# Decoder cross-attention: score matmuls and output copies issued in another order

## What is computed

```python
def _L1_xattn_ref(query, key, value, mask, Wq, bq, Wk, bk, Wv, bv, Wo, bo):   # key = value = ctx_1024
    q = (query @ Wq + bq).reshape(b, -1, H, HD).transpose(0, 2, 1, 3)
    k = (key @ Wk + bk).reshape(b, -1, H, HD).transpose(0, 2, 1, 3)
    v = (value @ Wv + bv).reshape(b, -1, H, HD).transpose(0, 2, 1, 3)
    scores = jnp.einsum('bhsd,bhtd->bhst', q, k) / jnp.sqrt(jnp.asarray(HD, q.dtype))
    scores = jnp.where(keep[None, None], scores, neg)
    w = jax.nn.softmax(scores, axis=-1)
    out = jnp.einsum('bhst,bhtd->bhsd', w, v)
    return out.transpose(0, 2, 1, 3).reshape(b, -1, D) @ Wo + bo
x = x + _L1_xattn_ref(_layernorm(x, axis=-1), ctx_1024, ctx_1024, mask_SxS2_ik0, ...)
```

## Time and profile before

| | |
|---|---|
| median of 3 runs | 3188.79 us (3188.61 to 3189.98) |
| the profiled execution, its own time | 3191.41 us |
| span of its trace | 3189.6 us |
| instructions | 37762 |
| PE busy | 2897.8 us (91% of the span) |
| DVE busy | 1304.7 us (41%) |
| ACT busy | 981.8 us (31%) |
| POOL busy | 247.2 us (8%) |

### The profile page before, as it was taken

The page is one execution under the profiler, slowest core; times in us unless marked ns, Lnnn a source line. Parts: engine busy times, 40 slices in busy tenths (PEclk is TensorE's granted clock), DMA queues, the critical chain, the costliest instruction groups (busy, mean ns, idle before and its releaser), DMA issues.

```text
span 3189.6 us, 37762 instructions
## 1 busy us (share of the span) xinstructions
PE 2897.8 (91%) x15710; PEld 2000.6 (63%) x15710; DVE 1304.7 (41%) x1979; ACT 981.8 (31%) x1469; POOL 247.2 (8%) x250
## 2 busy tenths in 40 slices
PE   7868899896998879999999979999999999987787
PEld 3336446354574458888888848778877877844422
DVE  3445363555741433333333342443344244246201
ACT  3233223123440234333443322332342243232100
POOL 1100110220000000000000011011101101000000
PEclk9989999997999979999999979999999999988899
DMA  9763794851021022222322210100100100021197
GB/s 385 289 274 109 306 378 188 357 225 40 14 76 47 24 80 94 104 92 94 104 92 93 104 69 21 44 23 21 44 24 21 44 24 21 24 113 40 57 422 298
DMA packets 62273, 388.87 MB, mean 122 GB/s; under 512 B 5696, under 2 KB 12096, under 8 KB 32704
## 3 DMA queue, kind: packets, MB, share of 16 engines
q1 hardware_dynamic: 26640, 190.57, 16.2%
q0 software_dynamic: 29024, 192.23, 15.3%
q10 hardware_dynamic: 6480, 4.20, 0.4%
HBM read 381.72 MB, written 5.24 MB: 121 GB/s over the span
## 4 chain that ended last, share of the span: by engine, by line
PE 68%; issue 10%; DMA 8%; DVE 8%; ACT 4%; POOL 2%; SPq 0%; DVEq 0%; ACTq 0%; POOLq 0%
PE PS L410 9%; PE PS L412 9%; PE PS L411 9%; PE PS L589 4%; PE PS L1644 4%; DMA PR<-in_ctxN 4%; PE PS L1625 3%; PE PS L1608 3%; PE PS L1626 3%; PE PS L1627 3%; PE PS L1610 3%; PE PS L1609 3%; PE PS L297 2%; DMA ring<-in_experts 2%; PE PS L564 2%
## 5 line engine op out<-in xcount | busy, mean ns | idle before, releaser
L410 PE MATMUL PS<-X_high,W_high 128*128 128x512 f32 x576 | 226.3, 393 | 14.5 <-DVE X_low L1124 7.3
L411 PE MATMUL PS<-X_low,W_high 128*128 128x512 f32 x576 | 225.8, 392 | 0.0
L412 PE MATMUL PS<-X_high,W_part 128*128 128x512 f32 x576 | 225.7, 392 | 0.0
L1106 DVE TENSOR_TENSOR W_part<-ring,W_high 128x2048 fp32r<-128x2048 f32 x63 | 147.0, 2334 | 188.6 <-ACT W_high L1072 188.6
L410 PE MATMUL PS<-H_high,W_high 128*128 128x512 f32 x576 | 224.1, 389 | 0.0
L411 PE MATMUL PS<-H_low,W_high 128*128 128x512 f32 x576 | 224.1, 389 | 0.0
L412 PE MATMUL PS<-H_high,W_part 128*128 128x512 f32 x576 | 224.1, 389 | 0.0
L1072 ACT ACTIVATE W_high<-ring 128x2048 fp32r<-128x2048 f32 x71 | 135.1, 1915 | 255.0 <-PE PS L412 255.0
L1808 DVE TENSOR_TENSOR RB<-PS,rows 128x512 f32<-128x512 f32 x104 | 71.9, 691 | 307.3 <-PE PS L1627 307.3
L1112 DVE TENSOR_TENSOR H_low<-T,H_high 128x512 fp32r<-128x512 f32 x144 | 99.7, 692 | 213.5 <-ACT H_high L1093 213.5
L1608 PE MATMUL PS<-C_high,W_part 128*128 128x384 f32 (+2 forms) x512 | 177.5, 347 | 4.9 <-DVE W_part L1780 4.9
(11 more groups left out here) (312 smaller groups left out, 5615.7 us busy)
## 6 DMA issues: line engine op xcount, KB each, us to landing
ring<-in_experts SPq DMA_DIRECT2D x96, 1024.0 KB, 4.9
ring<-in_tiles SPq DMA_DIRECT2D x39, 1024.0 KB, 4.9
RA<-in_ctxT POOLq DMA_DIRECT2D x20, 1792.0 KB, 9.1
RA<-in_ctxT POOLq DMA_DIRECT2D x20, 1536.0 KB, 7.3
T<-in_ctxN POOLq DMA_DIRECT2D x24, 1024.0 KB, 14.0
RA<-in_experts SPq DMA_DIRECT2D x24, 1024.0 KB, 12.8
RB<-in_ctxT POOLq DMA_DIRECT2D x12, 1792.0 KB, 15.6
RC<-in_ctxN POOLq DMA_DIRECT2D x12, 1792.0 KB, 12.3
```

Of the source, the lines that this page charges most:

```text
L410: pe.matmul(ps, a, xh, start=start, stop=False)
L411: pe.matmul(ps, a, xl, start=False, stop=False)
L412: return pe.matmul(ps, b, xh, start=False, stop=stop)
```

## The change

Nothing is added or taken away: the same instructions run on each engine, in another order. The first group's scores stay where they were. In `s4_pe`, `scores(b, g + 2, 0)` now stands between `values(b, g, 2)` and `values(b, g, 3)`, one group earlier in the loop's text, where it stood at the head of the next group as `scores(b, g + 1, 0)`. And `transposes(b, g, 1, 1)` now stands ahead of `scores(b, g + 1, 1)`. In `s4_dve`, `out(b, g)` was the last call of a group's round; it now stands in the next round, between the maxima of the first and of the second half.

```diff
@@ s4_pe
                 vals(b, 1, range(4, HALF[1][1]))
+                scores(b, 1, 0)
                 for g in range(KC):
-                    if g + 1 < KC:
-                        scores(b, g + 1, 0)
                     transposes(b, g, 0, 0)
                     transposes(b, g, 0, 1)
                     transposes(b, g, 1, 0)
+                    transposes(b, g, 1, 1)
                     if g + 1 < KC:
                         scores(b, g + 1, 1)
-                    transposes(b, g, 1, 1)
                     values(b, g, 0)
                     transposes(b, g, 2, 0)
                     transposes(b, g, 2, 1)
...
                     transposes(b, g, 3, 0)
                     transposes(b, g, 3, 1)
                     values(b, g, 2)
+                    if g + 2 < KC:
+                        scores(b, g + 2, 0)
                     if g + 1 == KC and b + 1 < B:
                         keys(b + 1, 0)
                     values(b, g, 3)
@@ s4_dve
                 for g in range(KC):
                     if g + 1 < KC:
-                        for h in (0, 1):
-                            maxima(b, g + 1, h, 0)
-                            maxima(b, g + 1, h, 1)
+                        maxima(b, g + 1, 0, 0)
+                        maxima(b, g + 1, 0, 1)
+                    if g:
+                        out(b, g - 1)
+                    if g + 1 < KC:
+                        maxima(b, g + 1, 1, 0)
+                        maxima(b, g + 1, 1, 1)
                     turn_out(b, g * 2 * NG + BY_DVE[0])
                     if g + 1 < KC:
                         normalise(b, g + 1, 0)
                     turn_out(b, g * 2 * NG + BY_DVE[1])
                     if g + 1 < KC:
                         normalise(b, g + 1, 1)
-                    out(b, g)
+                out(b, KC - 1)
```

## The result

| | median | runs | range |
|---|---|---|---|
| before | 3188.70 us | 6 | 3185.74 to 3193.14 |
| changed | 3175.89 us | 6 | 3172.74 to 3178.82 |

The ratio of the times is 0.996, with a 95% interval of 0.9947 to 0.9973: the change makes the kernel 0.4% faster, 12.8 us by the medians. The prediction was 3174 with a range of 3169.5 to 3181.

A forecast was written before the change was run, and what follows sets the result against it. TensorE, busy 91% of the span, was taken as the bound, through its rounds in stage 4. Gains of 0.79 + 0.83 + 0.22 = 1.84 us a batch, 14.7 over eight, took the median from 3188.79 to 3174, range 3169.5 to 3181.

The forecast's parts named there:

- Sixteen in one run should take 1.89: TensorE's transposes at a round's start: 0.15 + 0.109 us each, so 1.89 where 12 and 4 took 2.05.
- the chain: Second scores, maximum, exponential, then copies or reciprocal and scaling across three engines; sets round 2's end at 10.12 us.
- 0.58 + 0.05 + 0.20: Round 1, copy 4's start to `values` 2: the copy 0.58 us, release some 0.05, then the transpose, 6.99 to 7.19.
- the stall: Second `scores` call, heads 2 and 3 waiting for the second maxima: 2.26 us instead of 1.56, a loss of 0.70.
- Late next: Round 1, second of the two single transposes: a new wait of 0.30 us for bank 5, freed by copy 4.
- The unknown cost: Values directly behind scores, absent from the trace: 0 to 0.3 us a batch, 0 to 2.4 in all; nothing was taken.
- the lower bound: Values directly behind scores cost nothing beyond the 0.15 us that each run already pays.
- one more change of mode at 0.15: Scores between two value calls drain TensorE in two rounds a batch: gain 2.4 us smaller, median 3176.
- The stall did not stay: Rival: second scores stay stalled at 0.67 us because DVE is later than summed; gain 8.3, median 3180.5; 6%.
- the wait for copy 4 was not absent: Rival: the wait for copy 4 is partly absent, gain more than summed, median 3169 to 3171; 4%.
- the batch's border: Rival: time saved in the groups is waited for at a batch's border, no measurable gain, median 3189; 5%.
- the clock did not fall: Rival: TensorE's clock falls to 1.2 GHz in denser rounds, so slower, up to 120 us, median 3294; 3%.

The follow-up runs named there:

- experiment 4: Changed kernel with the first scores back at the head of their own round, behind the last values: 3187.90 us, 0.9988 of before.
- Experiments 1: Changed kernel with the moves of the four transposes and of the output copies undone, so only the first scores move: 3203.89 us, 1.0047 of before.
- experiment 3: Changed kernel with DVE's order as before, the output copies at the end of a round: 3192.09 us, 1.0002 of before.
- experiment 2: Changed kernel with the four transposes back behind the second scores: 3182.74 us, 0.9975 of before.
- experiment 5: Changed kernel with copy 4 on DVE and copy 5 on ACT, the other way round than before: 3176.78 us, 0.9947 of before.
- experiments 6 and 7: 6: changed kernel, round 2's second scores ahead of the four transposes, 3177.15 us; 7: the same plus copy 4 on DVE and copy 5 on ACT, 3173.99 us.
- experiment 8: The changed kernel, unaltered, timed again beside the other runs: 3178.74 us, 0.9959 of before.

## Why the prediction was right

**The bound and the method.** Rounds of one batch, priced by distances of starts and added over eight batches: the stage gave back 12.6 us, eight times 1.57. The sum said 14.7, eight times 1.84.

| | predicted | measured |
|---|---|---|
| round 0 | 10.14 | 10.25 |
| round 1 | 10.14 | 10.24 |
| round 2 to group 3's twelve | 10.12 | 10.17 |
| second scores, round 0 | 1.8 | 1.75 |
| second scores, rounds 1 and 2 | 1.56 | 1.55, 1.56 |
| sixteen transposes | 1.89 | 1.93 |
| copy 4's start to `values` 2 | 0.83 | 0.89 |

**What was mis-sized.** The 2.1 us that are missing lie in two small terms. "Sixteen in one run should take 1.89" was drawn from runs of 12 and fewer; it takes 1.93, and this stands ahead of the chain in all three rounds. And from copy 4 to `values` 2 the sum took 0.58 + 0.05 + 0.20, since it gave the second transpose half of the pair's 0.37. In the changed kernel `values` 2 come 0.26 after a transpose that had to wait, and so 0.58 + 0.05 + 0.26 = 0.89. Together 0.04 + 0.06 a round, against the 0.10 to 0.11 of rounds 0 and 1, and 0.04 of the 0.05 of round 2.

**The scores ahead of the last values** are the core, and the reason given (1.56 us of ready work fill the wait for the last copy) is shown by experiment 4: without them the wait ahead of the last values is back (0.47 us by the bracket, 0.55 by the starts), and 9 of the 12.6 us are gone.

**The output copies behind the first maxima** were priced as hidden, and they are (0.88 us to spare ahead of `values` 0, 0.7 expected). The prediction gave this part no share of the gain and did not say what would happen without it, though it said that the copies "leave the way of the first maxima". Experiments 1 and 3 show what this is worth: 11.7 us (845.6 - 833.9) and, without the transposes, 22.0 (857.8 - 835.8). The three parts don't add up one by one.

**The transposes ahead of the second scores** were said to remove the stall at the price of a later start. True in rounds 1 and 2, and it leaves 0.2 in round 0. But the stall was mostly a symptom: experiment 2 keeps all of it in round 0 (2.22) and some in rounds 1 and 2 (1.86), and loses only 1.9 us. What such a stall costs goes another way than through the maximum: it delays the four transposes behind the scores, so copy 3, so the exponential. In round 2 of before the exponential starts at 2250.17, directly behind copy 3, 0.62 later than its maximum would let it (2248.43 + 1.12). That is 4.91 into the round; it is 4.50 in experiment 2 and 4.73 in the change, where it follows the maximum. In round 2 the part even costs 0.23, which the sum did not set apart. No run tried the other way out, ACT's exponential ahead of copy 3.

**Late next.** The wait for copy 4 was forecast at 0.30 in round 1; it is 0.36 there (and 0.16 in round 0, where `values` 0 come later), and experiment 5 shows its cause. For round 2 a wait of 0.6 ahead of the last values was expected, and 0.54 was found, read in the same way.

**The unknown cost.** Values directly behind scores pay nothing extra: scores to values takes 1.55 (2236.20 to 2237.75), the last values 0.37, as the earlier trace rows have them elsewhere. So the lower bound was the right choice; the changes of tiling mode cost no more than the 0.15 that each run carries already. For one more change of mode at 0.15 the prediction worked out a median of 3176, and 3175.89 was measured, but that is chance: the rows show no such cost, and the 2.1 us are those of the two small terms above.

**The rivals.** The stall did not stay, the wait for copy 4 was not absent, the batch's border took nothing (the three rounds gained 0.68, 0.73 and 0.17, and the whole batch 1.57), and the clock did not fall. The window over the stage in the changed kernel (columns as the earlier trace rows):

```profile
1922.00:2822.00 900.00, 887.51 (x6275) 714.26 (x6273) 371.82 (x719) 304.49 (x481) 81.73 (x31) 1.00 0.08 29
```

## What to carry to other kernels

Where one engine's order is written by hand, look for ready work that stands right behind a wait and put it ahead; then check, on every other engine, that what this work feeds does not stand behind something that waits for what was passed. Here that second step, four small copies on an engine that is 59% idle, decided, with the transposes left in place, between 0.25% faster and 0.5% slower; with them moved as well, between 0.4% and nothing. Price such a change as a chain of starts over one round, and verify it by the length of the round in the trace: it repeats to 0.02 us here, where the times of one kernel's runs scatter by up to 13 us.

## What the runs showed of the hardware

- A `scores` call of eight matmuls (four heads side by side, two passes) takes 1.55 to 1.56 us when nothing is waited for. When its third head is held, the maximum of heads 0 and 1 is still ready no earlier than 1.67 after the call's start and 1.0 after the release. By these two numbers a stall below 0.67 us does not delay that maximum. In round 0 of the changed kernel it starts at 2221.23, 1.67 after the call's start at 2219.56, though the call is 0.2 longer; in round 2 of experiments 6 and 7 it comes after 1.67 too, with stalls of 0.31 and 0.42. With a stall of 0.70 (before) it comes after 1.71, and with 0.94 (experiment 3) after 1.94.
- Single transposes behind a wait. In round 2 of the changed kernel, on PE's timeline:

```profile
2244.68 0.33 PE L1661 MATMUL PS<-sq,PR 128*128 128x128 f32 x1
2245.16 0.33 PE L1661 MATMUL PS<-sq,PR 128*128 128x128 f32 x1
2245.42 1.09 PE L1675 MATMUL PS<-PTs,RB 128*64 128x128 f32 x16
```

The values follow 0.26 us after the second transpose, and again 0.26 in round 1 of experiment 8 (2237.70 to 2237.96); half of an unhindered pair's 0.37 would have been 0.19.
